# A state-space mixer: two of eight channel tiles convolved on TensorE by diagonal matrices, one gate piece and the step's positive part at other places of the turn

## The reference

```python
xz = jnp.einsum('bld,ed->ble', xn, in_proj_w)          # 512 -> 2 x 1024
x_inner, z = jnp.split(xz, 2, axis=-1)
xc = conv_general_dilated(x_inner^T, conv_w, padding=[(3, 0)], feature_group_count=1024)  # 4 taps, each channel by itself
xc = silu(xc + conv_b)
x_ssm = jnp.einsum('bld,ed->ble', xc, x_proj_w)        # 16 B, 16 C, 1 step
dt = softplus(x_ssm[..., -1:] * dt_w[:, 0] + dt_b)
h = exp(dt*A) * h + (dt*u) * B ; y = sum(h*C) + D*u    # scan over the tokens, 16 states a channel
out = einsum(y * silu(z), out_proj_w) + residual
```

## Time and profile before

| | |
|---|---|
| median of 3 runs | 3008.19 us (3007.95 to 3009.06) |
| the profiled execution | 3007.99 us, its span 3006.4 us |
| mixer (first exponential to last scan) | from 502.85 to about 1641.6 us of the span |
| one turn | 71.7 to 72.5 us |
| PE, DVE, ACT, POOL busy over the span | 82%, 64%, 47%, 40% |

### The profile page before, as it was taken

The page is one execution under the profiler, slowest core; times in us unless marked ns, Lnnn a source line. Parts: engine busy times, 40 slices in busy tenths (PEclk is TensorE's granted clock), DMA queues, the critical chain, the costliest instruction groups (busy, mean ns, idle before and its releaser), DMA issues. The chain is left out here.

```text
span 3006.4 us, 48030 instructions
## 1 busy us (share of the span) xinstructions
PE 2464.7 (82%) x17070; PEld 2086.0 (69%) x17071; DVE 1930.0 (64%) x2723; ACT 1407.9 (47%) x3465; POOL 1205.3 (40%) x757
## 2 busy tenths in 40 slices
PE   4999996788888888888887730699999689999986
PEld 4999996788878888888876520344444367777775
DVE  7566434999999999999998360122222257677653
ACT  0342327878888888888875210011111123333432
POOL 3100003666666666666665017200000345554331
PEclk9988978999999999999999855799999778899996
DMA  5700000000000110000000016456555321111000
GB/s 204 318 1 1 1 1 29 30 30 31 30 31 30 38 45 37 30 31 30 30 30 1 7 62 199 133 173 223 197 174 172 99 54 29 47 42 31 8 8 15
DMA packets 63511, 201.49 MB, mean 67 GB/s; under 512 B 12346, under 2 KB 17594, under 8 KB 60474
## 3 DMA queue, kind: packets, MB, share of 16 engines
q1 hardware_dynamic: 25210, 96.31, 9.3%
q0 software_dynamic: 26272, 80.77, 8.4%
q10 hardware_dynamic: 11808, 21.50, 1.9%
HBM read 130.31 MB, written 68.23 MB: 66 GB/s over the span
## 5 line engine op out<-in xcount | busy, mean ns | idle before, releaser
L841 POOL TENSOR_TENSOR m_hs<-m_hs,m_BC 128x1040 f32<-128x1040 f32 x256 | 619.0, 2418 | 381.8 <-DVE m_hs L954 381.8
L760 ACT ACTIVATE m_dA<-m_dt,m_A 128x128 f32<-128x128 f32 x2048 | 614.3, 393 | 185.1 <-DVE m_hs L954 110.5
L635 PE MATMUL m_py<-m_hs,ident 128*128 128x130 f32 x4096 | 530.1, 284 | 146.7 <-POOL m_hs L841 146.7
L954 DVE TENSOR_TENSOR_SCAN m_hs<-m_dA,m_own 128x1040 f32<-128x1040 f32 x256 | 593.2, 2317 | 35.5 <-ACT m_dA L760 22.3
L635 PEld LDWEIGHTS m_py<-m_hs,ident 128*128 128x128 f32 x4096 | 496.9, 197 | 166.2 <-POOL m_hs L841 164.0
L939 DVE TENSOR_TENSOR m_own<-m_BC,m_own 128x1040 f32<-128x1040 f32 x256 | 318.7, 1245 | 17.9 <-DVE m_own L911 3.2
L587 PE MATMUL m_pw<-m_xg,m_w_in 128*128 128x130 f32 x2048 | 273.7, 294 | 51.3 <-DVE m_xc L902 34.9
L587 PEld LDWEIGHTS m_pw<-m_xg,m_w_in 128*128 128x128 f32 x2048 | 264.9, 210 | 55.0 <-DVE m_xc L902 37.9
L1384 PE MATMUL e_pG<-e_w_gu,e_xT 128*128 x656 | 235.2, 502 | 10.9 <-issue 7.0
L1364 POOL DMA_DIRECT2D e_x<-slots x80 | 42.9, 536 | 403.1 <-PE e_pX L1375 396.3
L1384 PEld LDWEIGHTS e_pG<-e_w_gu,e_xT 128*128 128x128 f32 x656 | 119.7, 192 | 91.5 <-issue 25.3
(11 more groups left out here) (272 smaller groups left out, 4609.6 us busy)
## 6 DMA issues: line engine op xcount, KB each, us to landing
m_BC<-xs SPq DMA_DIRECT2D x16, 2080.0 KB, 10.0
slots<-a_zero POOLq DMA_DIRECT2D x48, 512.0 KB, 38.9
e_w_gu<-in_gate_up_w SPq DMA_DIRECT2D x32, 768.0 KB, 5.2
e_x<-slots POOLq DMA_DIRECT2D x82, 256.0 KB, 2.9
slots<-e_y ACTq DMA_DIRECT2D x82, 256.0 KB, 2.6
e_w_d<-in_down_w SPq DMA_DIRECT2D x32, 256.0 KB, 5.7
out_h<-t_ho SPq DMA_DIRECT2D x8, 520.0 KB, 3.3
a_AT<-in_A_cols SPq DMA_DIRECT2D x8, 512.0 KB, 7.0
```

Of the source, the lines that this page charges most:

```text
L635: mm = pe.matmul(py[k % 2][:, 0:MT], ident[:, :], hs[u % NB][:, n, :], start=False, stop=(half == 1 and n == HN - 1))
L760: act.activation(images(dA[u % NB][:, n, :])[:, :, 1:TOK], images(dt[b][:, k, :])[:, :, 1:TOK], ACT.Exp, scale=A[:, at:at + 1]).then_inc(d ...
L841: pool.tensor_tensor(hs[u % NB][:, :, :], hs[u % NB][:, :, :], BC[b][:, ST + half * HN:ST + (half + 1) * HN, :], ALU.mult).then_inc(prod_r ...
L954: dve.tensor_tensor_scan(hs[u % NB][:, :, :].rearrange("p n t -> p (n t)"), dA[u % NB][:, :, :].rearrange("p n t -> p (n t)"), bu, 0.0, AL ...
```

## The change

Three things. First, the tiles of the third piece (6 and 7) are no longer convolved by ACT and DVE: ACT copies their projection from PSUM to SBUF (`e1`) in one instruction, and PE, at its unit 3, multiplies it with four diagonal matrices a tile (`diag`, made at setup from the identity and the taps), shifted by a tap each, adding up in bank 2. `silus` then makes two silus of one tile each from that bank with the bias, and one silu of the other six tiles. Second, gate piece 2, which needs bank 2, waits for these two silus (`pw_free`) and is issued at PE's unit 5 instead of 4, in front of `x_proj`. Third, `relus` stands at ACT's unit 13 instead of 12. The buffer `lp` is gone: lp is put in the `dt` buffer that `relus` writes afterwards, so `relus` now waits for POOL's first logarithm step (`log_steps`). Turn 0's own input, convolved in the setup, keeps the old way.

```diff
+PE_TILES = PIECES[2]
+PE_CONV_AT = 3
-        lp = sb("lp", [P, ET, MT])
+        diag = sb("diag", [P, len(PE_TILES) * KC, P])
@@ in_piece (PE)
-                    pe.wait_ge(conv_ready, q * ET + PIECES[j][-1] + 1)
+                    if j == 2 and not first:
+                        pe.wait_ge(pw_free, q)
+                    else:
+                        pe.wait_ge(conv_ready, dve_tiles(q) + PIECES[j][-1] + 1)
@@ new (PE)
+            def conv(q):
+                pe.wait_ge(tap0, (q + 1) * ET)
+                for at in range(len(PE_TILES)):
+                    for s in range(KC):
+                        mm = pe.matmul(images(pw[2][:, at * MT:(at + 1) * MT])[:, :, s:TOK], diag[:, at * KC + s, :],
+                                       images(e1[:, at, :])[:, :, 0:TOK - s], start=(s == 0), stop=(s == KC - 1))
+                mm.then_inc(pe_conv, 1)
@@ turn (PE)
-                        if GATE_AT <= u < GATE_AT + NP:
+                        if u == PE_CONV_AT:
+                            if first:
+                                pe.wait_ge(diag_set, len(PE_TILES) * KC)
+                            conv(g + 1)
+                        if GATE_AT <= u < GATE_AT + NP - 1:
                             in_piece(g + 1, 1 - b, 1, u - GATE_AT)
+                        if u == GATE_AT + NP:
+                            in_piece(g + 1, 1 - b, 1, NP - 1)
@@ tap_piece (ACT)
+                if j == 2 and not first:
+                    n = len(PE_TILES)
+                    act.activation(e1[:, 0:n, :], pw[j][:, 0:n * MT].rearrange("p (j t) -> p j t", t=MT), ACT.Copy).then_inc(tap0, n)
+                    return
@@ silus (ACT)
-                act.wait_ge(conv_ready, (q + 1) * ET)
-                act.activation(xc[b][:, :, :], xc[b][:, :, :], ACT.Silu).then_inc(u_ready, 1)
+                    act.wait_ge(pe_conv, q)
+                    for at, e in enumerate(PE_TILES):
+                        silu = act.activation(xc[b][:, e, :], pw[2][:, at * MT:(at + 1) * MT], ACT.Silu, bias=conv_b[:, e:e + 1])
+                    silu.then_inc(pw_free, 1)
+                    act.wait_ge(conv_ready, dve_tiles(q) + DT)
+                    act.activation(xc[b][:, 0:DT, :], xc[b][:, 0:DT, :], ACT.Silu).then_inc(u_ready, 1)
@@ steps, relus (ACT)
-                act.activation(lp[:, :, :], e1[:, :, :], ACT.Identity, bias=-1.0).then_inc(ln_steps, 1)
+                act.activation(dt[b][:, :, :], e1[:, :, :], ACT.Identity, bias=-1.0).then_inc(ln_steps, 1)
+            def relus(q, b):
+                act.wait_ge(log_steps, q * 2 + 1)
-                        if u == STEP_AT + 1:
-                            relus(1 - b)
+                        if u == STEP_AT + 2:
+                            relus(g + 1, 1 - b)
@@ turn (DVE)
-                    elif not last and CONV_AT <= u < CONV_AT + NP:
+                    elif not last and CONV_AT <= u < CONV_AT + NP - 1:
                         conv_piece(g + 1, 1 - b, u - CONV_AT)
@@ setup (DVE)
+            for at, e in enumerate(PE_TILES):
+                for s in range(KC):
+                    dve.tensor_scalar(diag[:, at * KC + s, :], ident[:, :], conv_w[:, e, KC - 1 - s:KC - s], None, ALU.mult).then_inc(diag_set, 1)
```

More of the change, by code:

```diff
@@ L527, in mamba, with dve_tiles @@
         y_ready, out_done, h_ready = map(sem, ("y_ready", "out_done", "h_ready"))
+        diag_set, pe_conv, pw_free = map(sem, ("diag_set", "pe_conv", "pw_free"))
+        DT = ET - len(PE_TILES)
+        def dve_tiles(q):
+            return q * DT + len(PE_TILES) if not (isinstance(q, int) and q == 0) else 0
         block = ctx.enter_context(nc.Block())
@@ L700, in root, with tap_piece @@
                 act.activation(scale[:, :, :], scale[:, :, :], ACT.Exp, scale=-0.5).then_inc(scale_ready, 1)
-            def tap_piece(q, b, j):
+            def tap_piece(q, b, j, first=False):
                 act.wait_ge(in_done, q * 2 * NP + j + 1)
+                if j == 2 and not first:
+                    n = len(PE_TILES)
+                    act.activation(e1[:, 0:n, :], pw[j][:, 0:n * MT].rearrange("p (j t) -> p j t", t=MT), ACT.Copy).then_inc(tap0, n)
+                    return
                 for at, e in enumerate(PIECES[j]):
@@ L707, in tap_piece, with silus @@
                                    scale=conv_w[:, e, KC - 1:KC]).then_inc(tap0, 1)
-            def silus(q, b):
-                act.wait_ge(conv_ready, (q + 1) * ET)
-                act.activation(xc[b][:, :, :], xc[b][:, :, :], ACT.Silu).then_inc(u_ready, 1)
+            def silus(q, b, first=False):
+                if first:
+                    act.wait_ge(conv_ready, ET)
+                    act.activation(xc[b][:, :, :], xc[b][:, :, :], ACT.Silu).then_inc(u_ready, 1)
+                else:
+                    act.wait_ge(pe_conv, q)
[4 more added lines that the diff above has]
+                    act.activation(xc[b][:, 0:DT, :], xc[b][:, 0:DT, :], ACT.Silu).then_inc(u_ready, 1)
                 for j in range(NP):
@@ L724, in take_xs, with steps @@
                 act.activation(xs[:, :], pw[0][0:XP, 0:MT], ACT.Copy).then_inc(xs_ready, 1)
-            def steps(q, first=False):
+            def steps(q, b, first=False):
                 act.wait_ge(s_done, q + 1)
@@ L739, in steps @@
                 act.wait_ge(ln_steps, q * 4 + 2)
-                act.activation(lp[:, :, :], e1[:, :, :], ACT.Identity, bias=-1.0).then_inc(ln_steps, 1)
+                act.activation(dt[b][:, :, :], e1[:, :, :], ACT.Identity, bias=-1.0).then_inc(ln_steps, 1)
                 act.activation(e1[:, :, :], e1[:, :, :], ACT.Ln).then_inc(ln_steps, 1)
-            def relus(b):
+            def relus(q, b):
+                act.wait_ge(log_steps, q * 2 + 1)
                 for e in range(ET):
@@ L772, in turn @@
                         if u == STEP_AT:
-                            steps(g + 1)
+                            steps(g + 1, 1 - b)
                             if more:
@@ L786, in _ @@
             for j in range(NP):
-                tap_piece(0, 0, j)
-            silus(0, 0)
+                tap_piece(0, 0, j, first=True)
+            silus(0, 0, first=True)
             square(1)
@@ L792, in _ @@
             root(1)
-            steps(0, first=True)
-            relus(0)
+            steps(0, 0, first=True)
+            relus(0, 0)
             turn(0, 0, first=True)
@@ L824, in log_step @@
                     pool.wait_ge(ln_steps, q * 4 + 3)
-                    pool.tensor_tensor(ex[:, :, :], ex[:, :, :], lp[:, :, :], ALU.subtract).then_inc(log_steps, 1)
+                    pool.tensor_tensor(ex[:, :, :], ex[:, :, :], dt[b][:, :, :], ALU.subtract).then_inc(log_steps, 1)
                 elif step == 1:
@@ L895, in conv_piece @@
                 n = len(PIECES[j])
-                done = (q * ET + PIECES[j][0]) * (KC - 2)
+                done = (dve_tiles(q) + PIECES[j][0]) * (KC - 2)
                 for s in range(1, KC):
@@ L964, in turn @@
                     if not last:
-                        if CONV_AT <= u < CONV_AT + NP and half == 0:
+                        if CONV_AT <= u < CONV_AT + NP - 1 and half == 0:
                             conv_piece(g + 1, 1 - b, u - CONV_AT)
```

## The result

| | before | changed |
|---|---|---|
| median of 20 runs, us | 3009.05 (3005.65 to 3011.93) | 3002.76 (2995.51 to 3010.32) |
| ratio | | 0.998, 95% interval 0.9974 to 0.9987 |
| the profiled execution, us (span) | 3007.99 (3006.4) | 2995.84 (2994.2) |
| first scan of turn 0 to first scan of turn 15 | 1076.99 | 1069.42 |

The change saves 6.3 us, 0.2%; the interval of the ratio is 3.9 to 7.8 us. 7.2 us were forecast against the median shown then (3001.0 against 3008.19). The profiled execution of the changed kernel is one of the fastest of its twenty: its span is 12.2 us shorter, but only 7.57 us of that lie in the turns. 2.1 us lie ahead of them and 2.5 us behind, nearly all in stages that the change doesn't touch. So I compare turns.

A forecast was written before the change was run, and what follows sets the result against it. DVE bounds on average, ACT's chain between the scans of units 5 and 12. Gains of 0.40 us in twelve loop turns, 0.56 in two others, 1.44 in turn 14, less 0.2, make 7.1: 3001.0 us, range 2989 to 3010.

The forecast's parts named there:

- Part 1: DVE before unit 5's scan: six convolution instructions leave, scan 1.24 us earlier in loop turns, 1.40 outside the loop.
- Part 2: PE behind unit 3's sums: the convolution's 1.95 us lie in 2.34 us of idle time before gate piece 1; cost 0.
- Part 3: ACT's silus, PE's gate piece 2, ACT's last gate silu in a row: chain 4.59 us instead of 3.43, 1.16 longer.
- rival with a low clock: PE at gate piece 2: at 1.2 GHz it takes 1.95 us more in 15 turns, 3030 us; chance 0.04.
- Part 4: Positive part behind unit 13's exponentials: frees 1.05 us, 0.32 left as POOL's logarithm step holds DVE's scaling; 1.20 in turn 14.
- Part 5: Setup: new diagonal tiles cost 0 in DVE's waiting time; first positive part waits for POOL's first step, 0.2 us lost.
- The first rival: DVE's scaling after unit 13's scan is not held by POOL, or only slightly: 2990.5 us; chance 0.13.

The follow-up runs named there:

- the logarithm step early: Changed kernel with POOL's second logarithm step behind its unit 11 instead of 12; 2998.50 us.
- the positive part alone: Kernel before with only the positive part moved to ACT's unit 13 and lp kept in the dt buffer, convolution left on ACT and DVE; 3003.02 us.
- The early copy: Changed kernel, but ACT copies the two convolved tiles out of bank 2 at unit 8, gate piece 2 back at PE's unit 4, one silu of eight tiles; 2983.98 us.
- the positive part back: Changed kernel with the positive part back at ACT's unit 12 instead of 13; 3005.95 us.

## Why the prediction was right

**Part 1, DVE's third piece:** forecast 1.24 us a loop turn and 1.40 outside. Measured 1.25 (25.45 to 24.20) and, in turns 0, 13 and 14, 1.39, 1.42 and 1.41.

**Part 2, convolution on PE covered:** right for ordinary turns (1.94 us in an idle time that fell from 2.34 to 0.57). Wrong in the turns behind a jump in which the clock fell: there PE is late already, the convolution takes the slack that used to make it good, and the order of part 3 passes the delay on (this chain is read from the rows; no run changed the clock alone). In the profiled execution this cost 0.9 us (turns 5 and 9), with the logarithm step early 6 us. The prediction had a rival with a low clock, but at gate piece 2 itself, where the clock was 1.00.

The rows that this part rests on the earlier trace rows are of turn 5, and most turns weren't like it. In nine of turns 1 to 13 of the kernel before (1, 2 and 7 to 13) the clock fell behind the 2.3 us of idle time, and gate piece 1 took 4.4 to 4.6 us instead of 2.95; in the positive part alone it did so in all thirteen. In the changed kernel and all those made from it, with the convolution in that idle time, the granted clock there was 1.00 in every turn. Turn 7, before and changed, the piece and its stretch with the granted clock third from last:

```profile
1033.46 4.42 PE L587 MATMUL m_pw<-m_xg,m_w_in 128*128 128x130 f32 x24 [2.31 <-DVE m_xc L902]
1033.00:1038.00 5.00, 4.54 (x26) 4.54 (x27) 5.00 (x10) 0.39 (x2) 0.38 (x1) 0.67 0.01 2
```

```profile
1028.52 2.85 PE L598 MATMUL m_pw<-m_xg,m_w_in 128*128 128x130 f32 x24
1028.00:1033.00 5.00, 5.00 (x48) 5.00 (x47) 4.70 (x4) 1.28 (x5) 1.25 (x2) 1.00 0.02 5
```

It made no difference to the time: 5 to 12 was 27.65 us before the change with either length. So the place that lost the low clock is not the place that has it now, and whether the one has to do with the other no run shows.

**Part 3, ACT, PE, ACT:** forecast 1.16 us, measured 1.06 by the distances and 1.05 between the table loads. Of that 0.63 is the wait for PE and 0.42 ACT's own longer work; the prediction gave 0.45 for the latter. The early copy, which ends both, gave all of it back (27.66). The term is made of slightly wrong pieces: the two silus took 0.63 us, not 0.80, since the pace of the step's positive part doesn't fit them, and gate piece 2 took 2.06 us, not 1.95. The prediction had PE ready 0.2 us earlier than pw_free; in the trace they come together (silus done at 964.49, sums of unit 5 at 964.66, gate piece 2 from 964.54), so it isn't shown which of the two it waits for.

**Part 4, the positive part:** freed 1.05 us, 0.32 of it left by forecast, 0.33 measured; 1.20 in turn 14, measured 1.22. The held scaling ended 0.55 us after POOL's step, forecast 0.56. Three kernels with the step or the scaling elsewhere and two with the positive part back or alone show the cause. The GPSIMD Engine Reference of the Trainium skill, section 1 (Specifications), names this contention for two SBUF inputs; the traces agree and add the length: until POOL's operation ends.

**Part 5, setup:** forecast 0.2 us lost. From PE's first instruction of the mixer to the first scan it was 50.94 us instead of 50.37, 0.6 lost. The other 0.4 lie in the input projection (17.28 us instead of 16.93), and they don't belong to the change: in six kernels made from the changed one, with the same setup, it took 16.87 to 17.26 us, and all that is outside it took 33.63 to 33.66 us in the seven against 33.44 before, 0.2 more, as forecast. The eight diagonal tiles took 3.54 us beside two POOL operations, where the eight alike of `skip` took 1.65; all of it lies in waiting time.

**The sum:** 7.3 us in the turns forecast, 7.57 measured: 0.39 a loop turn on average against 0.40, 0.66 and 0.67 in turns 0 and 13 against 0.56, 1.56 in turn 14 against 1.44. That it lands within 0.3 us is in part luck. An ordinary turn of the loop gained 1.25 − 1.06 + 0.33 = 0.52 us, not 0.40, which would be 6.2 us in twelve. Against that stand two losses that the forecast hadn't: 0.9 us in turns 5 and 9, and 0.6 from unit 14 to the next unit 0 at the jumps. Another execution can have more or fewer late turns; with the logarithm step early they cost 6 us. The mechanism is shown term by term for ordinary turns; the agreement of the total is worth less than it looks. The first rival (no hold, 17.7 us) was the one that a reader of DVE's idle times alone would have forecast.

## What to carry to other kernels

When a wait of the bound engine is taken away, look at what that engine does next and whether it meets an operation of POOL there: an operation of DVE with two inputs in SBUF should be the first behind the instruction that releases POOL, or stand where POOL is idle. When work moves to another engine because that engine has idle time, keep the result out of a bank that the next step waits for; here two cheap copies in ACT's idle time were worth twice the whole change. Slack on an engine behind a loop's jump is what absorbed its late starts here, so it wasn't free to fill.

## What the runs showed of the hardware that I had not expected

Between DVE's operations with two inputs in SBUF and POOL's, whichever was there first ran, instruction by instruction: of two DVE operations in a row behind the same scan, the first (0.28 us) was in before POOL, and the second, 0.03 us too late, was held 2.2 us. Where a POOL operation ended with both DVE and another POOL operation waiting, DVE went first in every case that I looked at, and POOL's took longer (2.85 us instead of 2.40 behind the held scaling).

At the start of a turn PE's granted clock fell behind a loop's jump (0.60 to 0.88 over 8.5 us, mostly with a stretch at 0.50, the level of 1.2 GHz, in it), and mostly behind 1.4 to 2.2 us of idle time. In the twelve traces it fell there only in turns that stand first in an iteration, and not in all of those: in five of six iterations of one execution (the logarithm step early) and in none of another (the positive part alone, 1.6 us idle in turn 7). Turn 3 of the kernel before had 0.82 behind 1.9 us, its turn 7 had 1.00 behind 2.1 us. At the low clock 32 matmuls took up to 6.5 us instead of 3.7. Idle time that costs nothing in itself can thus carry a slow start of the engine behind it, as in front of gate piece 1 before the change (4.4 to 4.6 us instead of 2.95).
